# Expert results added into four sums by scatters, in place of one row for each token and place

## The reference

```python
def _L1_ffn_ref(x, centroids, expert_biases, Ws_up, Ws_down, W_up, W_down):
    TOP_K = 8                                   # D = 256, F = 128, E = 64
    xf = x.reshape(T, D)
    shared = silu(xf @ Ws_up) @ Ws_down
    aff = xf @ centroids.T
    _, idx = top_k(aff + expert_biases, TOP_K)
    w = sigmoid(take_along_axis(aff, idx, axis=1))
    w = w / (sum(w, axis=-1) + 1e-08)
    cw = zeros((T, E)).at[arange(T)[:, None], idx].add(w)
    h = silu(einsum('td,edf->etf', xf, W_up))
    y = einsum('etf,efd->etd', h, W_down)
    routed = einsum('etd,te->td', y, cw)
    return shared + routed
```

## Time and profile before

| | us |
|---|---|
| median of 3 runs | 1137.18 |
| lowest and highest | 1129.81, 1139.08 |
| the profiled execution | 1134.61 |
| its span, first to last instruction | 1132.8 |

### The profile page before, as it was taken

The page is one execution under the profiler, slowest core; times in us unless marked ns, Lnnn a source line. Parts: engine busy times, 40 slices in busy tenths (PEclk is TensorE's granted clock), DMA queues, the critical chain, the costliest instruction groups (busy, mean ns, idle before and its releaser), DMA issues.

```text
span 1132.8 us, 22500 instructions
## 1 busy us (share of the span) xinstructions
PE 904.2 (80%) x6292; PEld 762.9 (67%) x6292; DVE 558.8 (49%) x1926; ACT 394.3 (35%) x1376; POOL 407.4 (36%) x467
## 2 busy tenths in 40 slices
PE   5899997999999889888888886388787887778700
PEld 4788886899999767666666664276676776667600
DVE  4666665111111247676766664244434443443368
ACT  1222222211111345554545452044444444444300
POOL 3100001311110103565555545445555555555500
PEclk9899997899999969998989898599989898998855
DMA  7122235799999289222222222756565665565488
GB/s 232 66 98 100 99 112 189 242 329 332 326 322 315 92 221 304 96 92 91 94 90 94 89 83 96 251 182 194 186 185 180 192 190 177 188 187 179 136 350 330
DMA packets 126053, 207.08 MB, mean 183 GB/s; under 512 B 13440, under 2 KB 101376, under 8 KB 123904
## 3 DMA queue, kind: packets, MB, share of 16 engines
q1 hardware_dynamic: 101824, 145.01, 39.9%
q0 software_dynamic: 19712, 56.65, 13.8%
q10 hardware_dynamic: 4416, 4.20, 1.1%
HBM read 134.50 MB, written 71.30 MB: 182 GB/s over the span
## 4 chain that ended last, share of the span: by engine, by line
PE 62%; DVE 9%; another core or an unknown queue 8%; ACT 7%; issue 7%; DMA 3%; POOL 2%; DVEq 1%; SPq 0%; POOLq 0%; ACTq 0%
PE PS L724 10%; PE PS L959 9%; PE PS L972 7%; PE PS L734 5%; PE PS L945 3%; PE PS L597 3%; DVE R L1702 3%; ACT R L1145 3%; PE PS L615 3%; PE PS L797 3%; PE PS L844 2%; PE PS L807 2%; PE PS L786 2%; POOL queue L1793 2%
## 5 line engine op out<-in xcount | busy, mean ns | idle before, releaser
L1831 POOL DMA_INDIRECT routed<-Q,idx_y x192 | 185.9, 968 | 168.2 <-DVE w_col L1667 69.2
L959 PE MATMUL PS<-R,Q 128*128 x768 | 131.5, 298 | 60.7 <-ACT Q L1210 58.4
L959 PEld LDWEIGHTS PS<-R,Q 128*128 128x128 f32 x768 | 111.1, 208 | 88.0 <-issue 78.4
L1793 POOL DMA_INDIRECT queue<-Q,slot x128 | 125.7, 982 | 87.0 <-DVE slot L1555 55.2
L972 PE MATMUL PS<-R,Q 128*128 x384 | 125.7, 412 | 7.4 <-DVE Q L1673 5.2
L1145 ACT ACTIVATE R<-PS,nmax 128x154 f32<-128x154 f32 x256 | 108.2, 546 | 64.6 <-DVE nmax L1477 63.2
L724 PEld LDWEIGHTS PS<-R 128*128 128x128 f32 x1024 | 121.4, 195 | 4.6 <-issue 3.1
L724 PE MATMUL PS<-R 128*128 128x128 f32 x1024 | 122.0, 278 | 2.1 <-DMA R<-in_down 1.0
L1216 ACT ACTIVATE Q<-PS 128x128 f32<-128x128 f32 x192 | 53.4, 278 | 139.3 <-PE PS L959 68.7
L1673 DVE COPY Q<-PS 128x128 f32<-128x128 f32 x192 | 54.7, 285 | 91.5 <-PE PS L966 54.8
L1210 ACT ACTIVATE Q<-PS 128x256 f32<-128x256 f32 x192 | 74.2, 386 | 49.4 <-PE PS L945 34.5
(11 more groups left out here) (271 smaller groups left out, 1696.6 us busy)
## 6 DMA issues: line engine op xcount, KB each, us to landing
Q<-queue SPq DMA_DIRECT2D x192, 192.0 KB
R<-in_gate_up SPq DMA_DIRECT2D x32, 1024.0 KB
R<-in_down SPq DMA_DIRECT2D x32, 512.0 KB
R<-routed SPq DMA_DIRECT2D x16, 1024.0 KB, 18.8
queue<-pads SPq DMA_DIRECT2D x16, 768.0 KB, 3.6
R<-in_W_up SPq DMA_DIRECT2D x16, 512.0 KB
R<-in_W_down SPq DMA_DIRECT2D x8, 1024.0 KB
routed<-R SPq DMA_DIRECT2D x32, 128.0 KB
```

The lines of the kernel that those rows point to most:

```text
L959: i = pe.matmul(bank(2 + p)[:, 0:F1], x1T[:, p, c, :], w_up1[:, bass.ts(e, 1), c, :], start=(c == 0), stop=(c == KC - 1))
L1793: pool.indirect_dma_start(out=queue1, out_offset=bass.IndirectOffsetOnAxis(ap=slot1[:, t * TOP1 + k:t * TOP1 + k + 1], axis=0), in_=pay[:, ...
L1831: pool.indirect_dma_start(out=routed1, out_offset=bass.IndirectOffsetOnAxis(ap=idx_y[:, a:a + 1], axis=0), in_=y1[:, k], in_offset=None).t ...
```

## The change

Four DRAM tensors summed1_0 to summed1_3 take the place of routed1. Each has 128 dump rows and one row for each token. Tile j is scattered into sum j % 4, and the DMA adds to what stands there. Ahead of the scatter of tile j POOL waits until that of tile j - 4, which adds into the same sum, has landed. The sums are set to zero by four DMAs in the first stage, and POOL waits for them once. All eight results of a token have the same place now, so that a queue row carries it 16 times in place of 64 numbers (XW = 336, 1344 bytes), and `places` reads it from a fixed column. In the tail the loads come in four quarters of four token tiles, one load of 512 KB for each quarter and sum, in rows of 1 KB, and no load waits for a residual. DVE adds four parts in two steps.

```diff
-    XW = D + 2 * E1
+    ROWW = 16
+    XW = D + E1 + ROWW
-    SUMS = 8
+    SUMS = 4
-    routed1 = nc.dram_tensor("routed1", [DUMPS + TOK * TOP1, D], F32).ap()
+    summed1 = [nc.dram_tensor(f"summed1_{i}", [P + TOK, D], F32).ap() for i in range(SUMS)]
...
                 sp.dma_start(queue1_pads[:, at], pads[:, :].unsqueeze(1).broadcast_to([P, E1 // NT, XW])).then_inc(S("pads_in"), 16)
+                if t % (NT // SUMS) == 1:
+                    sp.dma_start(summed1[t // (NT // SUMS)].rearrange("(n p) d -> p n d", p=P),
+                                 pads[:, 0:D].unsqueeze(1).broadcast_to([P, 1 + NT, D])).then_inc(S("sums_zeroed1"), 16)
...
-            for t in range(NT):
-                if t >= SUMS:
-                    sp.wait_ge(S("final"), t - SUMS + 1)
-                sp.dma_start(sums1[:, t % SUMS], routed1[DUMPS + t * P * TOP1:DUMPS + (t + 1) * P * TOP1, :].rearrange("(p k) d -> p k d", k=TOP1)).then_inc(S(f"sums_in{t % SUMS}"), 16)
+            for i in range(4):
+                at = slice(i * NT // 4, (i + 1) * NT // 4)
+                for k in range(SUMS):
+                    sp.dma_start(sums1[:, k, at], summed1[k][P + i * TOK // 4:P + (i + 1) * TOK // 4, :].rearrange("(n p) d -> p n d", p=P)).then_inc(S(f"sums_in{i}"), 16)
...
-                dve.wait_ge(S("sel1"), nth("sel1", t + 1))
-                dve.tensor_tensor_scan(pay[:, s, D + E1:XW].bitcast(I32), row(sel, t), row(sel, t), place0[:, t:t + 1], ALU.add, ALU.max).then_inc(S("place1"), 1)
+                dve.tensor_copy(pay[:, s, D + E1:XW].bitcast(I32), place0[:, t:t + 1].broadcast_to([P, ROWW])).then_inc(S("place1"), 1)
...
-                dve.tensor_scalar(idx_y[:, a:a + 1], g1[:, k, bass.ds(e + (D + E1), 1)].bitcast(I32), dump_at[:, k:k + 1], None, ALU.max).then_inc(S("idx_y"), 1)
+                dve.tensor_scalar(idx_y[:, a:a + 1], g1[:, k, D + E1:D + E1 + 1].bitcast(I32), dump_at[:, :], None, ALU.max).then_inc(S("idx_y"), 1)
...
-                part = sums1[:, t % SUMS]
-                for i, k in enumerate((TOP1 // 2, TOP1 // 4, TOP1 // 8)):
+                part = sums1[:, :, t]
+                for i, k in enumerate((SUMS // 2, SUMS // 4)):
                     dve.tensor_tensor(part[:, 0:k], part[:, 0:k], part[:, k:2 * k], ALU.add).then_inc(S("summed"), 1)
...
+            pool.wait_ge(S("sums_zeroed1"), nth("sums_zeroed1", 16 * SUMS))
             for j in range(NX1):
                 k, a = j % RING, j % AHEAD
                 pool.wait_ge(S("idx_y"), nth("idx_y", j + 1))
                 pool.wait_ge(S(f"y1_{j % 2}"), nth(f"y1_{j % 2}", j // 2 + 1))
                 pool.sem_inc(S("waited_pool"), 1)
-                pool.indirect_dma_start(out=routed1, out_offset=bass.IndirectOffsetOnAxis(ap=idx_y[:, a:a + 1], axis=0),
-                                        in_=y1[:, k], in_offset=None).then_inc(S(f"placed{k}"), 16)
+                if j >= SUMS:
+                    before = (j - SUMS) % RING
+                    pool.wait_ge(S(f"placed{before}"), nth(f"placed{before}", 16 * ((j - SUMS) // RING + 1)))
+                pool.indirect_dma_start(out=summed1[j % SUMS], out_offset=bass.IndirectOffsetOnAxis(ap=idx_y[:, a:a + 1], axis=0),
+                                        in_=y1[:, k], in_offset=None, compute_op=ALU.add).then_inc(S(f"placed{k}"), 16)
```

More of the change, by code:

```diff
@@ L59, in build @@
     routed0 = nc.dram_tensor("routed0", [NX0 * P, D], F32).ap()
-    XW = D + 2 * E1
+    ROWW = 16
+    XW = D + E1 + ROWW
     PAY = 4
-    SUMS = 8
+    SUMS = 4
     QROWS = P + TOK
     FAR = float(1 << 15)
-    DUMPS = RING * P
     AHEAD = 16
     queue1 = nc.dram_tensor("queue1", [E1 * QROWS, XW], F32).ap()
-    routed1 = nc.dram_tensor("routed1", [DUMPS + TOK * TOP1, D], F32).ap()
+    summed1 = [nc.dram_tensor(f"summed1_{i}", [P + TOK, D], F32).ap() for i in range(SUMS)]
     ctx = ExitStack()
@@ L115, in build @@
             LATER[f"sums_in{i}"] = (f"w0_in{i}", 32 * NX0 // 4)
-        for i, (name, loads) in enumerate((("ctx_in", NB + 6), ("mask_in", 1), ("ffn0_in", 4), ("small1_in", 6))):
-            LATER[f"sums_in{4 + i}"] = (name, 16 * loads)
+        LATER["sums_zeroed1"] = ("mask_in", 16)
         for k in range(RING):
@@ L198, in build @@
         idx_y = sb("idx_y", [P, AHEAD], I32)
-        dump_at = sb("dump_at", [P, RING])
+        dump_at = sb("dump_at", [P, 1])
         pads = sb("pads", [P, XW])
@@ L288, in build @@
         active1, began1, row_at = q(NX1), q(NX1), q(NX1)
-        sums1 = R[:, 0:SUMS * TOP1 * D].rearrange("p (n k d) -> p n k d", n=SUMS, k=TOP1)
+        sums1 = R[:, 0:SUMS * NT * D].rearrange("p (k n d) -> p k n d", k=SUMS, n=NT)
         PS = ctx.enter_context(nc.psum_tensor("PS", [P, 8, BANK], F32))
@@ L1698, in _ @@
             for t in range(NT):
-                dve.wait_ge(S(f"sums_in{t % SUMS}"), nth(f"sums_in{t % SUMS}", 16 * (t // SUMS + 1)))
-                part = sums1[:, t % SUMS]
-                for i, k in enumerate((TOP1 // 2, TOP1 // 4, TOP1 // 8)):
+                dve.wait_ge(S(f"sums_in{t // (NT // 4)}"), nth(f"sums_in{t // (NT // 4)}", 16 * SUMS))
+                part = sums1[:, :, t]
+                for i, k in enumerate((SUMS // 2, SUMS // 4)):
                     dve.tensor_tensor(part[:, 0:k], part[:, 0:k], part[:, k:2 * k], ALU.add).then_inc(S("summed"), 1)
-                    dve.wait_ge(S("summed"), 3 * t + i + 1)
+                    dve.wait_ge(S("summed"), 2 * t + i + 1)
                 dve.scalar_tensor_tensor(X[:, t, :], part[:, 0], rstd_all[:, t:t + 1], X[:, t, :], ALU.mult, ALU.add).then_inc(S("final"), 1)
@@ L1726, in _ @@
             pool.iota(pos1[:, :], pattern=[[P, NX1]], base=-int(FAR), channel_multiplier=0, allow_small_or_imprecise_dtypes=True).then_inc(S("pool_const1"), 1)
-            pool.iota(dump_at[:, :], pattern=[[P, RING]], base=0, channel_multiplier=1, allow_small_or_imprecise_dtypes=True).then_inc(S("pool_const1"), 1)
-            pool.iota(place0[:, :], pattern=[[P * TOP1, NT]], base=DUMPS - 1, channel_multiplier=TOP1, allow_small_or_imprecise_dtypes=True).then_inc(S("pool_const1"), 1)
+            pool.iota(dump_at[:, :], pattern=[[0, 1]], base=0, channel_multiplier=1, allow_small_or_imprecise_dtypes=True).then_inc(S("pool_const1"), 1)
+            pool.iota(place0[:, :], pattern=[[P, NT]], base=P, channel_multiplier=1, allow_small_or_imprecise_dtypes=True).then_inc(S("pool_const1"), 1)
             pool.iota(expert_rep[:, :], pattern=[[0, P]], base=0, channel_multiplier=1, allow_small_or_imprecise_dtypes=True).then_inc(S("pool_const1"), 1)
```

## The result

After the change the kernel takes 1138.6 us (median of 17 runs, 1137.32 to 1146.65). The kernel before, measured beside it, took 1134.84 (17 runs, 1129.81 to 1142.04). The ratio is 1.0045, with 1.0025 to 1.0064 as its 95% interval: half a per cent slower, where 1% faster was forecast.

What follows compares the result with a forecast made beforehand. The prediction took a PE and ACT ring to bound the loop, POOL having 0.49 us to spare, with the tail behind it. Terms of -14.0 + 0.8 - 0.5 = -13.7 us gave 1122 us, range 1117 to 1127.

Steps and rivals of the forecast that it cites:

- First POOL's own time: Expert loop: an adding scatter costs POOL 0.97 us as a copy does, upper end twice that; no loop time lost.
- rival B: Expert loop: an adding scatter costs POOL twice, 2.24 us a tile, so the loop follows POOL: +93 us, 1215; chance 0.10.
- Second the landing: Expert scatters: an adding one lands in 2.8 to 7.0 us, taken as 3.2; hidden in the loop, 0.8 us in the tail.
- Rival A: Expert loop: POOL waits for the landing four back, slower than before from 7.3 us; at 8.0 us +46.7, 1169; chance 0.11.
- Third the traffic: DMA engines in the expert loop: share rises from 0.59 to 0.76, covered by loads running seven tiles ahead of PE.
- The cover: Expert loop: loads run seven tiles ahead of PE; cover gone where a scatter holds the DMA engines for 1.16 us.
- The tail, step by step: After the loop, first load to end: 38.5 us in place of 52.5, a gain of 14.0 with ends 12.7 and 16.0.
- Rival C: Tail: rows of 1 KB load at only 279 GB/s, so it gains 6 us, giving 1130; chance 0.17.
- Small parts: Layer 0 zeroing at 0, smaller queue scatters before the loop 0.5 us gained, scan turned copy nothing.
- Rival D: Expert scatters: the adding is a copy in time and traffic, so the tail alone counts, 1120; no chance of its own.

Runs made afterwards that it cites:

- experiment 4: Kernel after with scatters adding only 128 of 256 columns into sums of half the width: 1136.34 us, ratio 0.9885 to before; loop 354.0 us.
- experiment 1: Kernel after with scatters that copy in place of adding: 1132.54 us, ratio 0.9885 to before; in a second set 1114.82, 0.9818.
- experiment 2: Kernel before with its scatters adding, each into zeroed rows of its own, without a wait for an earlier scatter: 1164.65 us, ratio 1.0154 to before.
- experiment 3: Kernel after with eight sums, four of them read, each scatter waiting for the one eight back: 1149.02 us, ratio 1.0053 to before.
- set of 1004: The one set of runs in which the kernel before took 1004.44 us, not 1134 to 1148; the kernel after was not timed there.
- experiment 6: Kernel after with three sums in place of four: 1095.55 us where before takes 1004.44, ratio 1.0902; in another set 1135.08, ratio 1.0008.

## Why the prediction was wrong

**First POOL's own time**: this is the step that failed. I took 0.97 us for an adding scatter, from copies and gathers of several sizes and both directions, and wrote that neither size nor direction matters. For the size that holds with an add too, 1547 ns at rows of 1 KB and of 512 bytes (experiment 4). But no row there held an add, and the add costs POOL 0.578 us more (experiments 1 and 2). The rows that I called near differed from the disputed one in the only thing that mattered. With 1.85 us a tile against the loop's 1.757, the excess of 0.095 x 191 gives the 18.2 us.

This is rival B's mechanism. Its price, twice POOL's time, was too high: 1.6 times was measured. The break-even point that I worked out for B was 1.83 us a tile, and the 1.853 lies just behind it. That the kernel is nearly where it was is chance: two effects of 18.0 and 14.7 us with nothing in common happen to be almost equal. I had 0.10 on B for one time of 1215, and not on all prices between 1.27 and 2.24. A middle price would not have saved the forecast, since half way is 1.755, where nothing is lost yet. But each 0.01 us beyond 1.757 costs 191 x 0.01 = 1.9 us, and written as a line with the points 1.757 (loss begins) and 1.83 (gain is gone) the cost would have shown that half of the range eats into the gain and two fifths of it take all.

**Second the landing**: mis-sized by a little. 0.8 us was taken for the tail and 1.4 came (2.49 to 3.89). The range of 2.8 to 7.0 held it. Rival A did not come: POOL waits for no landing, and two sums show where the chain begins to count.

**Third the traffic**: mis-sized. I had a share of 0.76 and 0.94 came; the pass for the add was priced at 0.38 us and it is 0.75 (1.09 less 0.34). The cover, gone at 1.16 us, held by 0.07. Since the loop runs at 353.8 to 354.1 with the engines at 0.73, 0.94 and 0.95 (experiments 4, 3 and 2), this term costs the time nothing. Had POOL been as fast as I thought, the engines would have been 0.94 x 1.853 / 1.757 = 0.99 busy by this estimate, and close to the next bound. The Trainium skill, Collectives: The Full Stack, section "The bandwidth ceiling", has the halved rate for the reduce step of a large ring transfer, and the prediction carried it over to a scatter. By it the scatters would have held 39.2%, twice a copy's share. The trace shows 58.9%, three times, and 38.6% at half the bytes. The direction holds here and the factor does not.

**The tail, step by step**: right. 38.5 was forecast and 37.8 measured, 36.5 to 39.8 being its ends. The pace inside a quarter is 1.59 for 1.62. The DMA engines are full (1.00) and the two waits at borders are 0.73 and 0.64 us, so they set the pace by a little, as worked out. From 1102 to 1120 us, while the loads run, the rate was 361 GB/s, inside my 346 to 366 (the 332 of the window from 1100 includes the start of the first load). One step was not as written: SP did not issue all loads at once. It needs 20.37 us for the 16, from 0.38 for the first to a median of 1.42, and the chain that ended last runs over these issues. At half the bytes and as many rows the median is 0.78 (experiment 4), so an issue seems to wait for the transfer of earlier loads, which leaves the DMA engines as the pace, and the sum holds. Rival C did not come.

**Small parts.** The zeroing at 0 was right. Its DMAs landed in 10.2 us, where I had 6.4 for the transfer alone, the share in that stage rose from 0.28 to 0.43, and the first scatter of layer 1 comes at 741.9 for 742.1. The 0.5 us of the queue rows wasn't seen: the piece at the loop's head is 5.79 for 5.83. The scan that became a copy takes 0.17 us for 0.35 and changes nothing.

**Rival D** (a copy in time and traffic) is excluded: where the scatters really copy (experiment 1) the loop is 18 us shorter and the landing 1.4 than in the kernel after.

So -14.7 + 1.4 + 18.0 stands in place of -14.0 + 0.8 - 0.5 + 0. The tail was right, two small terms were off by about half a microsecond each, and the loop, which I had at nothing, lost more than the tail gave.

## What to carry to other kernels

A change that gives an instruction a new mode has no near row: write its cost as a line, mark where it crosses the slack of its engine, and put the chances on the line. Here the slack was 0.49 us a tile and the add took 0.58. Before letting the DMA add, compare what it saves at the end, once, with what it costs POOL on every tile, and count that slack where the kernel runs fastest, not on the mean. In the set of 1004 the slack of before was nearly nothing by the estimate above, and adding into three sums cost 9%.

## What the runs showed of the hardware beyond that

- An adding scatter of 128 rows holds POOL 1.547 us against 0.969 for a copy, at 1 KB and at 512 bytes alike. At 1 KB it holds the DMA engines 1.09 us against 0.34, and lands in 3.8 us against 2.4.
- Its packets have 910 bytes on average, and 456 at half the columns (7.08 MB in 15529), where a copy's have 2.7 KB. 15533 packets in 200 us at 1.853 us a scatter are 144 for each, 16 more than it has rows.
- The same program takes 1134 to 1148 us in six sets and 1004 in one. In the set of 1004 layer 1's attention is where the kernels with the add are shorter: it begins at the same place (404.8 for 405.8 us, first activation of line 1147), and the scatters of the experts begin at 701 to 706 us in place of 740 to 753. PE was granted the full clock there. This is the window of three sums in the set of 1004 (experiment 6):

```profile
450.00:650.00 200.00, 187.89 (x1634) 144.24 (x1634) 156.84 (x441) 120.78 (x535) 131.35 (x149) 1.00 0.28 100
```

The kernel after has 171.48 us and 1369 instructions of PE in the same window, at 0.91. All four kernels profiled in the set of 1004 have 1.00 there, and all others 0.87 to 0.93. So the shorter time goes with the clock, but which of them is the cause, and what sets them apart, stays open. The record gives chip number 7 for this set and for that of experiments 1 to 4, in which before takes 1144. If the number stands for one chip, then the chip alone is not what makes the difference.
